# Scores and gates of a mixture of experts turned by VectorE instead of TensorE, with products over six PSUM banks

## The chip, the cores and the metric

The kernel runs on one core of a Trainium2 chip. The metric is the device time of one execution in microseconds (us). The engines are named as in the profile: PE is TensorE (PEld its weight loads), DVE is VectorE, ACT is ScalarE, POOL is GpSimd, SP is SyncE, which here only issues transfers. PSUM has eight banks of 512 fp32 numbers a partition.

## The reference

```python
x = x + L0_ffn(L0_cond(x, ..., itok_B_2_6), ...)     # gated FFN with per-sample adapters, then a linear layer
x = x + L1_ffn(L1_cond(x, W, b, coeff, mask), A, B, Wr)

def L1_ffn(x, A, B, Wr):           # 64 experts of rank 16, the top 16 of each token count
    scores = xf @ Wr.T                                    # 1024 tokens x 64 experts
    top_vals, top_idx = jax.lax.top_k(scores, 16)
    G = zeros(N, 64).at[rows, top_idx].set(softmax(top_vals))
    h = jnp.einsum('nd,krd->nkr', xf, A)                  # 1024 x 1024
    return 2.0 * jnp.einsum('nkr,kdr->nd', h * G[:, :, None], B)
```

x is 8 x 128 x 512 in fp32. The change touches only the scores, the gates G and the order around `h * G`.

## The kernel before, in words

Everything is kept features-first: a feature or an expert is a partition, a token a column. Each fp32 operand of a large product is split into a high and a low part, and `mm3` multiplies high by high, high by low and low by high (lines 1157 to 1159), so that a product over the depth of 512 (four blocks of 128) is 12 matmuls of 512 columns. ACT makes the high part by a copy (all its copies have line 479), DVE the low part by a subtraction (`low`, line 780), except that POOL makes the low part of the expert weights (`am_low`, line 462, and `bm_low`, line 467).

The end of the kernel, around the change, goes as follows. The order of each engine's queue is written out by hand, and engines wait for each other by semaphores.

- `cond(b)`, for the eight samples, writes bank 0 or 1; DVE adds a bias (`c_bias`, line 1011); PE turns the result in four transposes (`turn`, line 1386) into bank 2 or 3; ACT and DVE split it (`ct_high`, `ct_low`) into `c_hl`.
- `scores(s)` (line 1399), for the two halves s of 512 tokens, multiplies with the router's weights into bank 4. High and low halves of the weights lie beside each other, so 128 rows come out: 64 experts from the high part, 64 from the low part. ACT copies the bank into `s_sb` (`s_copy`). `turn_scores(s)` (line 1408) turns it, four tiles of 128 tokens, by products with `ident2`, two identities on top of each other, which also adds the two 64s. The result lies in bank 5, tokens on partitions.
- DVE copies the scores out (line 1030) and routes: `route_first8` takes the eight largest per token (MAX8, line 1032), subtracts the largest (line 1035, for the exponential that ACT makes in `exponent`, line 671) and strikes the eight out (line 1038); `route_next8` does so with the next eight (lines 1043 to 1048); `route_gates` multiplies, sums and inverts (lines 1052 to 1054), and scales the gates into `gate2`, each twice, in four instructions (line 1058). Within it each step waits for the one before.
- `turn_gates(s)` (line 1417) turns `gate2` in four PE transposes into bank 6, and `gate_copy(s)` (ACT) copies that to `gate_x`: 128 rows of gates, the 64 experts twice.
- `experts(n)`, n from 0 to 15, is a product of 12 matmuls with tile j of the expert weights for half s. `H_ORDER` goes over tiles 0 to 3 for half 0, tiles 0 to 3 for half 1, tiles 4 to 7 for half 0, and tiles 4 to 7 for half 1. The banks are 0 to 3 in turn. Four slots hold split weights (`AM_SLOTS`), so `am_high(4)` on ACT, then `am_low(4)` on POOL, must come before `experts(8)`. `hg_gate(n)` (DVE, line 1114) multiplies the bank with `gate_x` of its half, and `hg_high` (ACT) and `hg_low` (DVE) split the result. `combine` then multiplies with the second expert weights, DVE adds to x (line 1143), and the result is stored.

The queue of ACT behind the last samples reads, in this order: `ct_high(7)`, `exponent(0)`, `am_high(2)`, `am_high(3)`, `s_copy(1)`, `gate_copy(0)`, `exponent(1)`, `hg_high(0)` to `(3)`, `gate_copy(1)`, and then in a loop `am_high(n)` (n from 4 to 7), `hg_high(n)`. SP loads expert tile j + 2 when POOL is done with tile j.

Of the kernel before, what the change touches and what calls it, by code (L numbers as in the profile page):

```python
# [28 lines left out]
F32 = mybir.dt.float32  # L29
F32R = mybir.dt.float32r  # L30
I32 = mybir.dt.int32
ALU = mybir.AluOpType
# [3 lines left out]
P = 128  # L36
BATCH, SEQ, D = 8, 128, 512
T = BATCH * SEQ
KD = D // P
# [29 lines left out]

AM_SLOTS = 4  # L70
H_ORDER = [(j + dj, s) for j in range(0, JT, AM_SLOTS) for s in range(2) for dj in range(AM_SLOTS)]
HALF_TAIL = len(H_ORDER) - AM_SLOTS
LAST_TILES = (JT - 2, JT - 1)
# [3 lines left out]
def build(nc, x_blocks, small_in, mask_w, w_open, w_gu, w_dn, a_gu, a_dn, b_three, b_gu, b_dn,  # L77
          lora_a, lora_b, w0_t, w1_t, bias1, wr_t, a_moe, b_moe, consts, out):
    with ExitStack() as ctx:
# [17 lines left out]

        const_sb = at("const_sb", [P, 464], F32, R_CONST)
        block_mask = const_sb[:, 0:PAIR]
        ident = const_sb[:, PAIR:PAIR + P]  # L100
        ident2 = const_sb[:, PAIR + P:PAIR + P + EXPERTS]
        bias0_sb = const_sb[:, 448:448 + KD]
        lora_w_sb = const_sb[:, 448 + KD:448 + KD + 1]
        coeff_sb = const_sb[:, 448 + KD + 1:448 + KD + 1 + BATCH]
        small = R_CONST + 464 * 4
        small_sb = at("small_sb", [P, 64], I32, small)
# [69 lines left out]
        expo = at("expo", [P, 4, EXPERTS], F32, R_AD + 15 * KB)  # L176
        gate2 = at("gate2", [P, 4, 2, EXPERTS], F32, R_ACT + 54 * KB)
        gate_x = at("gate_x", [P, 2, HALF], F32, R_AD)
# [53 lines left out]
        wr_hi, wr_lo = sem("wr_hi"), sem("wr_lo")  # L232
        s_ready, s_copied, score_ready = sem("s_ready"), sem("s_copied"), sem("score_ready")
        top_step, shifted, exp_done, gate_done = sem("top_step"), sem("shifted"), sem("exp_done"), sem("gate_done")
        gate_tr, late_banks_free = sem("gate_tr"), sem("late_banks_free")
        am_hi, am_lo, h_ready, hg_mul, hg_hi, hg_lo = (sem("am_hi"), sem("am_lo"), sem("h_ready"), sem("hg_mul"),
# [34 lines left out]
        def _(sp):  # L271
# [26 lines left out]
            for b in range(4, 6):  # L298
                load_a(b, dma_a[1])
            sp.dma_start(const_sb[:, PAIR:464], consts[:, PAIR:464]).then_inc(dma_const, 16)  # L300

# [175 lines left out]
        def _(act_e):  # L477
# [187 lines left out]
            def s_copy(s):  # L665
                act_e.wait_ge(s_ready, s + 1)
                copy(s_sb[:], ps[:, 4]).then_inc(s_copied, 1)

# [4 lines left out]
            def gate_copy(s):  # L673
                act_e.wait_ge(gate_tr, s + 1)
                copy(gate_x[:, s], ps[:, 6]).then_inc(late_banks_free, 2)

# [66 lines left out]
            ct_high(BATCH - 1)  # L743
            exponent(0)
            am_high(2)
            am_high(3)

            def hg_high(n):
# [9 lines left out]

            s_copy(1)
            gate_copy(0)  # L760
            exponent(1)
            for n in range(4):
                hg_high(n)
# [14 lines left out]
        def _(dve):  # L778
# [247 lines left out]


            def route_first8(s):
                dve.wait_ge(score_ready, s + 1)
                step(nc.vector.tensor_copy(score[:], ps[:, 5, 0:4 * EXPERTS].rearrange("p (t e) -> p t e", t=4)))  # L1030
                for t in range(4):
                    last = nc.vector.max(top8[:, t, 0], score[:, t])
                step(last)

                nc.vector.tensor_tensor(expo[:], score[:], top8[:, :, 0, 0:1].broadcast_to([P, 4, EXPERTS]),
                                        ALU.subtract).then_inc(shifted, 1)
                for t in range(4):
                    last = nc.vector.match_replace(left1[:, t], top8[:, t, 0], score[:, t], NEG)
                step(last)
# [10 lines left out]
            def route_gates(s):  # L1050
                dve.wait_ge(exp_done, s + 1)
                step(nc.vector.tensor_tensor(left1[:], expo[:], left2[:], ALU.mult))
                step(nc.vector.tensor_reduce(gate_sum[:], left1[:], AX_X, ALU.add))
                step(nc.vector.reciprocal(gate_inv[:], gate_sum[:]))
                if s:
                    dve.wait_ge(gate_tr, s)
                for t in range(4):
                    last = nc.vector.tensor_scalar(
                        gate2[:, t], left1[:, t].unsqueeze(1).broadcast_to([P, 2, EXPERTS]),
                        gate_inv[:, t:t + 1], MOE_SCALE, ALU.mult, ALU.mult)  # L1060
                last.then_inc(gate_done, 1)

# [27 lines left out]
            for b in range(BATCH):  # L1090
                c_bias(b)
                if b + 2 < BATCH:
                    xs_low(b + 2)
                if b == 5:
                    wc_low_half(7, 0)
                    wc_low_half(7, 1)
                if b:
                    ct_low(b - 1)
                if 1 <= b < 5:
                    wc_low_half(5 + (b - 1) // 2, (b - 1) % 2)  # L1100
                if b == 6:
                    route_first8(0)
            ct_low(BATCH - 1)
            route_next8()
            route_gates(0)

            def hg_gate(n):
                j, s = H_ORDER[n]
                dve.wait_ge(h_ready, n + 1)
                dve.wait_ge(late_banks_free, 2 * (s + 1))  # L1110
                if n >= 2:
                    dve.wait_ge(hg_hi, n - 1)
                    dve.wait_ge(hg_lo, n - 1)
                nc.vector.tensor_tensor(hg_raw[:, n % 2], ps[:, n % 4], gate_x[:, s],
                                        ALU.mult).then_inc(hg_mul, 1)
# [39 lines left out]
        def _(pe):  # L1155
# [234 lines left out]
            def scores(s):  # L1390

                pe.wait_ge(ct_hi, 4 * s + 4)
                pe.wait_ge(ct_lo, 4 * s + 4)
                pe.wait_ge(x2_done, 2 * KD)
                pe.wait_ge(wr_hi, 1)
                pe.wait_ge(wr_lo, 1)
                for k in range(KD):
# [6 lines left out]
            def turn_scores(s):  # L1404

                pe.wait_ge(s_copied, s + 1)
                for t in range(4):
                    last = nc.tensor.matmul(ps[:, 5, t * EXPERTS:(t + 1) * EXPERTS], s_sb[:, t * P:t * P + P],  # L1408
                                            ident2, start=True, stop=True)
                last.then_inc(score_ready, 1)  # L1410

            def turn_gates(s):
                pe.wait_ge(gate_done, s + 1)
                if s:
                    pe.wait_ge(late_banks_free, 2)
                for t in range(4):
                    last = nc.tensor.transpose(ps[:, 6, t * P:t * P + P],  # L1417
                                               gate2[:, t].rearrange("p c e -> p (c e)"), ident)
                last.then_inc(gate_tr, 1)

            def experts(n, part=range(KD)):
                j, s = H_ORDER[n]
                pe.wait_ge(am_hi, j + 1)
                pe.wait_ge(am_lo, j + 1)
                if n >= 4:
                    pe.wait_ge(hg_mul, n - 3)
                for k in part:
                    last = mm3(ps[:, n % 4], am_hl[:, j % AM_SLOTS, 0, k], am_hl[:, j % AM_SLOTS, 1, k],
                               c_hl[:, 0, k, halves(s)], c_hl[:, 1, k, halves(s)], k == 0, k == KD - 1)
# [4 lines left out]
            for b in range(1, BATCH):  # L1434
# [18 lines left out]
            experts(5)  # L1453
            turn_gates(1)
            for n in range(6, 2 * JT):
# [16 lines left out]
            for o in range(KD):  # L1472
# [3 lines left out]
                for s in range(2):  # L1476
                    pe.wait_ge(late_banks_free, 2 * o + s + 1)
                    pe.wait_ge(hg_lo, HALF_TAIL + AM_SLOTS * s)
# [8 lines left out]
def constants():  # L1487
# [3 lines left out]
    eye = np.eye(P)  # L1491
    return np.concatenate([LORA_SCALE * own, eye, eye[:, :EXPERTS] + eye[:, EXPERTS:]], 1).astype(np.float32)

# [76 lines left out]
```

## Time and profile before

| | before |
|---|---|
| median of 3 runs | 354.89 us (354.57 to 354.99) |
| the profiled execution, whole time | 354.69 us |
| its span, first to last instruction | 353.0 us |
| PE busy | 349.5 us, 99% |
| PEld busy | 294.4 us, 83% |
| DVE busy | 202.2 us, 57% |
| ACT busy | 144.1 us, 41% |
| POOL busy | 78.0 us, 22% |

Times in the trace count from the start of the span. A timeline row gives the start, the duration, engine, line, operation, tile written and tiles read, their shape, and how many instructions are merged in it; in brackets stands how long the engine sat idle before it and what ended that. Matmuls overlap: one of 512 columns lasts 0.39 us in the trace, and the next starts about 0.23 us after it.

### The profile page before, as it was taken

Reading aid. Unit: us, or ns where it says so; the run is one execution under the profiler, and the core shown is the slowest. Engines: PE = TensorE matmul, PEld = TensorE weight load, DVE = VectorE, ACT = ScalarE, POOL = GpSimd, SP = SyncE. Lnnn points to the kernel's source line nnn. Section 1 sums busy time; section 2 is a strip of 40 time slices with the busy share of each in tenths; the row PEclk is TensorE's granted clock in tenths of the full one; section 3 lists DMA queues with packets and bytes.
Section 4 is the critical chain, followed back from the end, with each engine's and each line's share of the span. In section 5 each row is a group of like instructions: output and inputs, shape, how many; then the busy total and the mean of one; then the engine's idle time right before and its main releaser. Section 6 shows DMA issues by size and latency. Waiting matters only on the chain.

```text
span 353.0 us, 4621 instructions
## 1 busy us (share of the span) xinstructions
PE 349.5 (99%) x1682; PEld 294.4 (83%) x1682; DVE 202.2 (57%) x302; ACT 144.1 (41%) x196; POOL 78.0 (22%) x86
## 2 busy tenths in 40 slices
PE   8999999999999999999999999999999999999997
PEld 8899888888888888888888898888888888888885
DVE  3788755334533453685674565879888878501102
ACT  5577544422442243545464471566352443201100
POOL 2361657863340004000000000000041154002200
PEclk9999999999999999999999999999999999999999
DMA  7943343232120054297219019010052022101011
GB/s 202 323 126 144 114 138 112 78 104 77 52 80 0 0 177 130 79 395 291 59 35 306 3 22 417 38 52 11 0 177 62 0 61 69 51 32 59 30 61 59
DMA packets 14802, 37.31 MB, mean 106 GB/s; under 512 B 2272, under 2 KB 4224, under 8 KB 13504
## 3 DMA queue, kind: packets, MB, share of 16 engines
q1 hardware_dynamic: 11920, 31.18, 25.9%
q0 software_dynamic: 2432, 5.57, 5.5%
q10 hardware_dynamic: 432, 0.33, 0.3%
q8 instruction: 11, 0.18, 0.2%
q14 instruction: 7, 0.06, 0.1%
HBM read 34.97 MB, written 2.10 MB: 105 GB/s over the span
## 4 chain that ended last, share of the span: by engine, by line
PE 99%; DVE 0%; issue 0%
PE ps L1157 29%; PE ps L1158 29%; PE ps L1159 29%; PE ps L1179 3%; PE ps L1309 3%; PE ps L1399 1%; PE ps L1386 1%; PE ps L1194 1%; PE ps L1187 1%; PE ps L1198 1%; PE ps L1202 1%; PE ps L1234 1%; PE ps L1408 0%; PE ps L1417 0%; DVE x L1149 0%
## 5 line engine op out<-in xcount | busy, mean ns | idle before, releaser
L1158 PE MATMUL ps<-x_hl,w_hl 128*128 128x512 f32 x144 | 56.2, 390 | 0.0
L1157 PE MATMUL ps<-x_hl,w_hl 128*128 128x512 f32 x144 | 56.2, 390 | 0.0
L1159 PE MATMUL ps<-x_hl,w_hl 128*128 128x512 f32 x144 | 56.1, 389 | 0.0
L462 POOL TENSOR_TENSOR am_hl<-am_raw,am_hl 128x512 fp32r<-128x512 f32 x8 | 11.0, 1387 | 137.4 <-ACT am_hl L479 137.4
L418 POOL DMA_INDIRECT b_raw<-b_gu,row_of x32 | 32.1, 1003 | 27.7 <-DVE b_st L780 19.6
L800 DVE TENSOR_TENSOR glu<-glu,ps 128x512 f32<-128x512 f32 (+1 forms) x22 | 14.9, 683 | 38.8 <-ACT glu L511 26.0
L1159 PEld LDWEIGHTS ps<-x_hl,w_hl 128*128 128x128 f32 x144 | 27.1, 188 | 5.7
L511 ACT ACTIVATE glu<-ps 128x512 f32<-128x512 f32 (+1 forms) x22 | 12.8, 588 | 46.0 <-PE ps L1179 45.8
L1157 PEld LDWEIGHTS ps<-x_hl,w_hl 128*128 128x128 f32 x144 | 27.1, 188 | 5.4
L1158 PEld LDWEIGHTS ps<-x_hl,w_hl 128*128 128x128 f32 x144 | 27.1, 188 | 5.2
L1158 PE MATMUL ps<-act,wd_hl 128*128 128x512 f32 x80 | 31.2, 390 | 0.0
L1157 PE MATMUL ps<-act,wd_hl 128*128 128x512 f32 x80 | 31.2, 389 | 0.0
L1159 PE MATMUL ps<-act,wd_hl 128*128 128x512 f32 x80 | 31.2, 389 | 0.0
L1143 DVE TENSOR_TENSOR x<-ps,x 128x512 f32<-128x512 f32 x8 | 5.5, 692 | 35.2 <-PE ps L1159 35.2
L1157 PE MATMUL ps<-c_hl,am_hl 128*128 128x512 f32 x64 | 25.3, 396 | 0.0
L1158 PE MATMUL ps<-hg,bm_hl 128*128 128x512 f32 (+2 forms) x66 | 25.3, 384 | 0.0
L1159 PE MATMUL ps<-hg,bm_hl 128*128 128x512 f32 (+2 forms) x66 | 25.3, 383 | 0.0
L1157 PE MATMUL ps<-hg,bm_hl 128*128 128x512 f32 (+2 forms) x66 | 25.3, 383 | 0.0
L1159 PE MATMUL ps<-c_hl,am_hl 128*128 128x512 f32 x64 | 25.0, 390 | 0.0
L1158 PE MATMUL ps<-c_hl,am_hl 128*128 128x512 f32 x64 | 24.9, 390 | 0.0
L780 DVE TENSOR_TENSOR act<-glu,act 128x512 f32 (+2 forms) x22 | 15.6, 711 | 16.3 <-ACT act L479 16.1
L989 DVE TENSOR_TENSOR wc_raw<-wc_raw,w_raw 128x2048 f32<-128x2048 f32 x8 | 18.3, 2292 | 7.4 <-ACT wc_raw L630 7.4
(151 smaller groups left out, 729.0 us busy)
## 6 DMA issues: line engine op xcount, KB each, us to landing
wc_raw<-mask_w SPq DMA_DIRECT2D x8, 1024.0 KB, 7.0
w_raw<-w_gu SPq DMA_DIRECT2D x8, 512.0 KB, 3.3
wd_raw<-w_dn SPq DMA_DIRECT2D x10, 256.0 KB, 2.7
w_raw<-w_t SPq DMA_DIRECT2D x2, 1024.0 KB, 7.3
x<-x_blocks SPq DMA_DIRECT2D x2, 1024.0 KB, 6.3
am_raw<-a_moe SPq DMA_DIRECT2D x8, 256.0 KB, 2.8
bm_raw<-b_moe SPq DMA_DIRECT2D x4, 512.0 KB, 3.6
x_raw<-x_blocks SPq DMA_DIRECT2D x7, 256.0 KB, 6.7
```

Of the source, the lines that this page charges most:

```text
L418: nc.gpsimd.indirect_dma_start(b_raw[f % 2][0:F_LAST, p].rearrange("q m f -> q (m f)"), None, b_gu, bass.IndirectOffsetOnAxis(ap=row_of[0: ...
L462: nc.gpsimd.tensor_tensor(am_hl[:, j % AM_SLOTS, 1], am_raw[:, j % 2], am_hl[:, j % AM_SLOTS, 0].bitcast(F32), ALU.subtract).then_inc(am_l ...
L511: nc.scalar.activation(glu[rows, slot], ps[rows, bank], ACT.Silu).then_inc(silu_done, 1)
L780: return nc.vector.tensor_tensor(out, whole, high.bitcast(F32), ALU.subtract)
L800: nc.vector.tensor_tensor(glu[rows, slot], glu[rows, slot], ps[rows, bank], ALU.mult).then_inc(glu_done, 1)
L989: nc.vector.tensor_tensor(wc[:], wc[:], w1_raw[:], ALU.add).then_inc(wc_added, 1)
L1143: nc.vector.tensor_tensor(x2[:, o, half], ps[:, 4 + n % 4], x2[:, o, half], ALU.add)\
L1157: nc.tensor.matmul(out, w_high, m_high, start=start, stop=False)
L1158: nc.tensor.matmul(out, w_high, m_low, start=False, stop=False)
L1159: return nc.tensor.matmul(out, w_low, m_high, start=False, stop=stop)
L1179: last = nc.tensor.matmul(ps[0:cols, bank, h * PAIR:h * PAIR + PAIR], stack[0:F_LAST, 2 * s + h, m, 0:cols], t_st[0:F_LAST, 2 * s + h, m], ...
L1309: last = nc.tensor.matmul(ps[:, 4 + g], stack, act_part(f, h, g * HALF, HALF)[rows], start=(n == 0 and h == 0), stop=(n == FT - 1 and h == 1))
```

## The change: what it does

- **Scores.** `turn_scores` on PE is gone, with `ident2` and 64 columns of constants. ACT copies only rows 64 to 127 of bank 4. DVE adds rows 0 to 63 of the bank to them (`sum_scores`) and turns the sum itself by 32x32 blocks: for each 32 experts four instructions, each of 32 partitions and 4 x 32 columns (`turn_scores`, now DVE's). For half 0 the first 32 experts are turned behind the sum, at b == 6, and the other 32 after `ct_low(7)`; `route_first8(0)`, which stood at b == 6, stands behind them.
- **Gates.** `turn_gates` on PE is gone. DVE scales the gates in one instruction into `gate_tok` (single, no longer twice), and turns them in eight instructions straight into rows 0 to 63 of `gate_x`. `gate_copy` copies these to rows 64 to 127.
- **Banks.** With banks 5 and 6 free, `experts(n)` goes over six banks, 0, 1, 2, 3, 6, 7, and waits for `hg_gate(n - 6)` instead of `hg_gate(n - 4)`.
- **Order.** On DVE `route_first8(1)` moves behind `hg_gate(0)` and `(1)`, and `hg_gate(3)` moves ahead of `route_gates(1)`. On ACT `am_high(2)` and `(3)` stand ahead of `exponent(0)`, and `hg_high(0)` and `(1)` ahead of `exponent(1)`.

```diff
+BLOCK = 32
+H_BANKS = (0, 1, 2, 3, 6, 7)
             def s_copy(s):
                 act_e.wait_ge(s_ready, s + 1)
-                copy(s_sb[:], ps[:, 4]).then_inc(s_copied, 1)
+                copy(s_sb[EXPERTS:P], ps[EXPERTS:P, 4]).then_inc(s_copied, 1)
             def gate_copy(s):
-                act_e.wait_ge(gate_tr, s + 1)
-                copy(gate_x[:, s], ps[:, 6]).then_inc(late_banks_free, 2)
+                act_e.wait_ge(gate_turned, s + 1)
+                copy(gate_x[EXPERTS:P, s], gate_x[0:EXPERTS, s]).then_inc(late_banks_free, 2)
...
             ct_high(BATCH - 1)
-            exponent(0)
             am_high(2)
             am_high(3)
+            exponent(0)
...
             s_copy(1)
             gate_copy(0)
+            for n in range(2):
+                hg_high(n)
             exponent(1)
-            for n in range(4):
+            for n in range(2, 4):
                 hg_high(n)
             gate_copy(1)
...
+            def sum_scores(s):
+                dve.wait_ge(s_copied, s + 1)
+                nc.vector.tensor_tensor(s_sb[0:EXPERTS], ps[0:EXPERTS, 4], s_sb[EXPERTS:P], ALU.add).then_inc(s_summed, 1)
+                dve.wait_ge(s_summed, s + 1)
+
+            def turn_scores(e):
+                summed = s_sb[e:e + BLOCK].rearrange("p (t q n) -> p t q n", t=4, n=BLOCK)
+                for q in range(P // BLOCK):
+                    last = nc.vector.transpose(score[q * BLOCK:q * BLOCK + BLOCK, :, e:e + BLOCK], summed[:, :, q])
+                step(last)
             def route_first8(s):
-                dve.wait_ge(score_ready, s + 1)
-                step(nc.vector.tensor_copy(score[:], ps[:, 5, 0:4 * EXPERTS].rearrange("p (t e) -> p t e", t=4)))
...
-                if s:
-                    dve.wait_ge(gate_tr, s)
-                for t in range(4):
-                    last = nc.vector.tensor_scalar(
-                        gate2[:, t], left1[:, t].unsqueeze(1).broadcast_to([P, 2, EXPERTS]),
-                        gate_inv[:, t:t + 1], MOE_SCALE, ALU.mult, ALU.mult)
-                last.then_inc(gate_done, 1)
+                step(nc.vector.scalar_tensor_tensor(gate_tok[:], left1[:], MOE_SCALE,
+                                                    gate_inv[:].unsqueeze(2).broadcast_to([P, 4, EXPERTS]),
+                                                    ALU.mult, ALU.mult))
+                for e in range(0, EXPERTS, BLOCK):
+                    turned = gate_x[e:e + BLOCK, s].rearrange("p (t q n) -> p t q n", t=4, n=BLOCK)
+                    for q in range(P // BLOCK):
+                        last = nc.vector.transpose(turned[:, :, q],
+                                                   gate_tok[q * BLOCK:q * BLOCK + BLOCK, :, e:e + BLOCK])
+                last.then_inc(gate_turned, 1)
...
                 if b == 6:
-                    route_first8(0)
+                    sum_scores(0)
+                    turn_scores(0)
             ct_low(BATCH - 1)
+            turn_scores(BLOCK)
+            route_first8(0)
             route_next8()
             route_gates(0)
...
-            route_first8(1)
+            sum_scores(1)
+            for e in range(0, EXPERTS, BLOCK):
+                turn_scores(e)
             hg_gate(0)
             hg_gate(1)
+            route_first8(1)
             hg_low(0)
             route_next8()
             hg_low(1)
             hg_gate(2)
+            hg_gate(3)
             route_gates(1)
             hg_low(2)
-            hg_gate(3)
             hg_low(3)
...
             def experts(n, part=range(KD)):
-                if n >= 4:
-                    pe.wait_ge(hg_mul, n - 3)
+                if n >= len(H_BANKS):
+                    pe.wait_ge(hg_mul, n - len(H_BANKS) + 1)
...
                 turn(b - 1)
-                if b == 6:
-                    turn_scores(0)
...
             experts(1)
-            turn_scores(1)
-            turn_gates(0)
             pe.wait_ge(ct_lo, BATCH)
             experts(2)
             experts(3)
             experts(4)
             experts(5)
-            turn_gates(1)
```

## Rows read from the trace of the kernel before

**Rows 1.** The page: busy time, and the chain that ended last.

```profile
PE 349.5 (99%) x1682; PEld 294.4 (83%) x1682; DVE 202.2 (57%) x302; ACT 144.1 (41%) x196; POOL 78.0 (22%) x86
...
PE 99%; DVE 0%; issue 0%
```

**Rows 2.** Windows: stage, busy time of PE, PEld, DVE, ACT, POOL, clock, DMA.

```profile
249.00:267.00 18.00, 18.00 (x95) 15.11 (x94) 15.31 (x45) 7.89 (x13) 5.58 (x4) 1.00 0.31 103
```

**Rows 3.** PE's timeline around the eight pieces that are removed.

```profile
251.17 0.60 PE L1386 MATMUL ps<-const_sb,c_tok 128*128 128x128 f32 x4
...
251.84 0.39 PE L1158 MATMUL ps<-wc_hl,xs_hl 128*128 128x512 f32 x1
...
254.37 0.60 PE L1386 MATMUL ps<-const_sb,c_tok 128*128 128x128 f32 x4
...
255.93 0.40 PE L1158 MATMUL ps<-wc_hl,xs_hl 128*128 128x512 f32 x1
...
266.43 0.39 PE L1159 MATMUL ps<-c_hl,am_hl 128*128 128x512 f32 x1
...
268.17 0.39 PE L1158 MATMUL ps<-c_hl,am_hl 128*128 128x512 f32 x1
...
278.64 0.39 PE L1159 MATMUL ps<-c_hl,am_hl 128*128 128x512 f32 x1
...
279.54 0.40 PE L1158 MATMUL ps<-c_hl,am_hl 128*128 128x512 f32 x1
```

**Rows 4.** PE's timeline: `turn(7)`, and the first matmul of `experts(8)`.

```profile
259.61 0.60 PE L1386 MATMUL ps<-const_sb,c_tok 128*128 128x128 f32 x4
...
284.80 0.39 PE L1157 MATMUL ps<-c_hl,am_hl 128*128 128x512 f32 x1
```

**Rows 5.** ACT's timeline: the second `gate_copy`.

```profile
279.56 0.60 ACT L479 ACTIVATE gate_x<-ps 128x512 f32<-128x512 f32 x1 [0.46 <-PE ps L1417]
```

**Rows 6.** POOL's timeline: `am_low(0)` and `(1)` together, then `am_low(4)`.

```profile
256.20 2.73 POOL L462 TENSOR_TENSOR am_hl<-am_raw,am_hl 128x512 fp32r<-128x512 f32 x2 [114.57 <-ACT am_hl L479]
...
280.76 1.30 POOL L462 TENSOR_TENSOR am_hl<-am_raw,am_hl 128x512 fp32r<-128x512 f32 x1 [14.73 <-ACT am_hl L479]
```

**Rows 7.** DVE's timeline, from the first scores to the second gates.

```profile
256.24 0.41 DVE L1030 COPY score<-ps 128x256 f32<-128x256 f32 x1
...
258.73 0.69 DVE L1011 TENSOR_TENSOR c_tok<-ps,bias_sb 128x512 f32<-128x512 f32 x1 [0.16 <-DVE left L1038]
...
260.88 0.69 DVE L780 TENSOR_TENSOR c_hl<-ps,c_hl 128x512 fp32r<-128x512 f32 x1 [0.45 <-ACT c_hl L479]
...
263.48 1.40 DVE L1052 TENSOR_TENSOR left<-expo,left 128x256 f32<-128x256 f32 x1
...
268.15 0.61 DVE L1032 MAX8 top<-score 128x8 f32<-128x64 f32 x4
...
270.03 1.29 DVE L1114 TENSOR_TENSOR hg_raw<-ps,gate_x 128x512 f32<-128x512 f32 x2
...
272.03 0.60 DVE L1043 MAX8 top<-left 128x8 f32<-128x64 f32 x4
...
274.03 0.69 DVE L780 TENSOR_TENSOR hg<-hg_raw,hg 128x512 fp32r<-128x512 f32 x1
274.64 0.68 DVE L1114 TENSOR_TENSOR hg_raw<-ps,gate_x 128x512 f32<-128x512 f32 x1
275.24 0.42 DVE L1052 TENSOR_TENSOR left<-expo,left 128x256 f32<-128x256 f32 x1
275.69 0.42 DVE L1053 TENSOR_REDUCE gate_sum<-left 128x4 f32<-128x256 f32 x1
...
276.36 0.88 DVE L1058 TENSOR_SCALAR gate<-left,gate_inv 128x128 f32<-128x128 f32 x4
```

**Rows 8.** Line 1058 by itself: durations in ns, least, median, most.

```profile
L1058 DVE TENSOR_SCALAR gate<-left,gate_inv x8: 274/280/531, 265.6 to 277.0; 128x128 f32<-128x128 f32 x8
```

**Rows 9.** The tile `am_raw`: DMA time from issue to landing.

```profile
DMA to landing us min/median/max: 2.5/2.8/4.2
```

More of the change, by code:

```diff
@@ L96, in build @@
         assert base + R_ACT + 88 * KB <= nc.sbuf_usable_end
-        const_sb = at("const_sb", [P, 464], F32, R_CONST)
+        const_sb = at("const_sb", [P, 400], F32, R_CONST)
         block_mask = const_sb[:, 0:PAIR]
         ident = const_sb[:, PAIR:PAIR + P]
[L101 to L105, printed above, removed]
+        bias0_sb = const_sb[:, PAIR + P:PAIR + P + KD]
+        lora_w_sb = const_sb[:, PAIR + P + KD:PAIR + P + KD + 1]
+        coeff_sb = const_sb[:, PAIR + P + KD + 1:PAIR + P + KD + 1 + BATCH]
+        small = R_CONST + 400 * 4
         small_sb = at("small_sb", [P, 64], I32, small)
@@ L176, in build @@
         expo = at("expo", [P, 4, EXPERTS], F32, R_AD + 15 * KB)
-        gate2 = at("gate2", [P, 4, 2, EXPERTS], F32, R_ACT + 54 * KB)
+        gate_tok = at("gate_tok", [P, 4, EXPERTS], F32, R_ACT + 54 * KB)
         gate_x = at("gate_x", [P, 2, HALF], F32, R_AD)
@@ L232, in build @@
         wr_hi, wr_lo = sem("wr_hi"), sem("wr_lo")
-        s_ready, s_copied, score_ready = sem("s_ready"), sem("s_copied"), sem("score_ready")
-        top_step, shifted, exp_done, gate_done = sem("top_step"), sem("shifted"), sem("exp_done"), sem("gate_done")
-        gate_tr, late_banks_free = sem("gate_tr"), sem("late_banks_free")
+        s_ready, s_copied, s_summed = sem("s_ready"), sem("s_copied"), sem("s_summed")
+        top_step, shifted, exp_done = sem("top_step"), sem("shifted"), sem("exp_done")
+        gate_turned, late_banks_free = sem("gate_turned"), sem("late_banks_free")
         am_hi, am_lo, h_ready, hg_mul, hg_hi, hg_lo = (sem("am_hi"), sem("am_lo"), sem("h_ready"), sem("hg_mul"),
@@ L299, in _ @@
                 load_a(b, dma_a[1])
-            sp.dma_start(const_sb[:, PAIR:464], consts[:, PAIR:464]).then_inc(dma_const, 16)
+            sp.dma_start(const_sb[:, PAIR:400], consts[:, PAIR:400]).then_inc(dma_const, 16)
             def load_tile(f, slot):
@@ L1113, in hg_gate @@
                     dve.wait_ge(hg_lo, n - 1)
-                nc.vector.tensor_tensor(hg_raw[:, n % 2], ps[:, n % 4], gate_x[:, s],
+                nc.vector.tensor_tensor(hg_raw[:, n % 2], ps[:, H_BANKS[n % len(H_BANKS)]], gate_x[:, s],
                                         ALU.mult).then_inc(hg_mul, 1)
@@ L1396, in scores @@
                 pe.wait_ge(wr_lo, 1)
+                if s:
+                    pe.wait_ge(s_summed, s)
                 for k in range(KD):
@@ L1402, in scores @@
                 last.then_inc(s_ready, 1)
[L1404 to L1419, printed above, removed]
             def experts(n, part=range(KD)):
@@ L1424, in experts @@
                 pe.wait_ge(am_lo, j + 1)
-                if n >= 4:
-                    pe.wait_ge(hg_mul, n - 3)
+                if n >= len(H_BANKS):
+                    pe.wait_ge(hg_mul, n - len(H_BANKS) + 1)
                 for k in part:
-                    last = mm3(ps[:, n % 4], am_hl[:, j % AM_SLOTS, 0, k], am_hl[:, j % AM_SLOTS, 1, k],
+                    last = mm3(ps[:, H_BANKS[n % len(H_BANKS)]], am_hl[:, j % AM_SLOTS, 0, k], am_hl[:, j % AM_SLOTS, 1, k],
                                c_hl[:, 0, k, halves(s)], c_hl[:, 1, k, halves(s)], k == 0, k == KD - 1)
@@ L1476, in _ @@
                 for s in range(2):
-                    pe.wait_ge(late_banks_free, 2 * o + s + 1)
+                    pe.wait_ge(late_banks_free, max(4, 2 * o + s + 1))
                     pe.wait_ge(hg_lo, HALF_TAIL + AM_SLOTS * s)
@@ L1491, in constants @@
     eye = np.eye(P)
-    return np.concatenate([LORA_SCALE * own, eye, eye[:, :EXPERTS] + eye[:, EXPERTS:]], 1).astype(np.float32)
+    return np.concatenate([LORA_SCALE * own, eye], 1).astype(np.float32)
 def rows_of_tiles():
@@ L1558 @@
         "b_moe": a["L1_ffn_B"].transpose(2, 0, 1).reshape(JT, P, KD, P).transpose(2, 1, 0, 3),
-        "consts": columns(464, [constants(), a["L0_ffn_bias"].reshape(KD, P).T,
+        "consts": columns(400, [constants(), a["L0_ffn_bias"].reshape(KD, P).T,
                                 np.repeat(a["L0_ffn_lora_weights"], RANK).reshape(P, 1),
```

## The prediction, as it was put on record before the result was known

> **What bounds the kernel now.** I read the page first, for the engine that is never free, then windows of the end of the kernel, then the timelines of PE, DVE, ACT and POOL there. The page shows PE busy for 99% of the span, and the chain that ended last is 99% PE [rows 1]. The window around the router shows the same: PE 18.00 us of 18.00 at a granted clock of 1.00, the 2.4 GHz level, although DVE is busy for 15.31 us there [rows 2]. So before the change nobody makes PE wait, an instruction taken off PE is worth its time, and one added to DVE costs nothing until it makes PE wait. The question is whether it will: DVE has only 2.7 us free in these 18.
>
> **What PE loses.** I measure each piece as a distance of starts against the same distance without it [rows 3].
> - `turn_scores(0)`: from the start of `turn` to the second matmul behind it is 255.93 - 254.37 = 1.56 us with it, and 251.84 - 251.17 = 0.67 us without. It is worth 0.89 us.
> - `turn_scores(1)` with `turn_gates(0)`: from the last matmul of one product to the second of the next is 268.17 - 266.43 = 1.74 us; two ordinary steps are 0.46. Worth 1.28 us.
> - `turn_gates(1)`: 279.54 - 278.64 = 0.90, less 0.46, is 0.44 us.
>
> Together 2.61 us. If nothing else moved, `experts(8)`, which starts at 284.80 [rows 4], would start at 282.19.
>
> **What `experts(8)` waits for.** It is the first product that needs expert tile 4. ACT makes the high part of that tile behind `gate_copy(1)` in its queue, and POOL the low part. Before, `gate_copy(1)` starts at 279.56 [rows 5] and POOL ends `am_low(4)` at 280.76 + 1.30 = 282.06 [rows 6], 2.74 us ahead of the matmul that wants it. These 2.74 us are all the room there is; taking 2.61 us of PE work away uses nearly all of it. Whatever delays `gate_copy(1)` then delays PE, one for one, and behind it stand `am_high(4)`, POOL's `am_low(4)` and SP's load of tile 6. So I follow the second gates through DVE.
>
> **What one turning instruction costs.** The trace has none. I need the distance T from one to the next in a row of them, each 128 columns. Bounds:
> - Four MAX8 over 64 columns take 0.61 us, 0.15 us each: half the columns, so a floor [rows 7].
> - Four TENSOR_SCALAR over 128 columns, which read and write as many elements per partition, take 0.88 us; one lasts 0.28, so the distance is (0.88 - 0.28) / 3 = 0.20 us [rows 7, 8].
> - The same instruction without any overlap is 0.28 us [rows 8]; and if a turned element took twice the time of a copied one, the distance would be about that of a 256-column instruction, 0.45 us with its wait [rows 7].
>
> I take 0.235 us. The nearest row is the one at 0.20, and a block of 32 columns must have come in before its first turned column can go out: from 256 to 512 columns an instruction grows by 0.69 - 0.42 = 0.27 us [rows 7], 1.05 ns a column, so 32 columns are 0.034 us, an estimate. One instruction then lasts 0.31 us, and a group of four with the wait behind it 3 x 0.235 + 0.31 + 0.04 = 1.055 us. The Trainium skill (VectorE: DVE Perf Modes, "The three transpose paths") gives 311 ns for a 128 x 128 bf16 turn on VectorE; no run here shows it, and by it the sum below would hardly change.
>
> **The path of the second gates, after.** All from [rows 7] unless another group is named.
> - `turn(7)` comes to PE 0.89 us earlier, at 258.72 instead of 259.61 [rows 4]. Its `c_bias(7)` stands on DVE behind the new `sum_scores(0)` and four turns. The sum starts at 256.24 where the copy of the scores stood, costs 0.73 (a 512-column instruction of 0.69 and the wait), the turns 1.055: `c_bias(7)` runs from 258.03 to 258.72. In the trace PE starts 0.19 us behind it (259.61 - 258.73 - 0.69), so PE stands at 258.91, a stall of 0.19. `ct_low(7)` moves with it by -0.70, to 260.18.
> - From there on DVE works without a pause. `ct_low(7)` 0.61, so 260.79; the other four turns 1.055; `route_first8(0)` without its copy 1.88 (270.03 - 268.15); `route_next8` 2.00 (274.03 - 272.03); multiply, sum, invert 1.12 (276.36 - 275.24); scale in one instruction 0.45 (as 275.69 - 275.24) in place of four of 0.88; eight turns 8 x 0.235 = 1.88. That is 269.18.
> - `sum_scores(1)` 0.73; two groups of turns 2.11; `hg_gate(0)` and `(1)` 1.20; `route_first8(1)` 1.88; `hg_low(0)` 0.61; `route_next8` 2.00; `hg_low(1)` 0.61; `hg_gate(2)` and `(3)` 1.20; 1.12 and 0.45 again: 281.09. Eight turns to the end of the last, 7 x 0.235 + 0.31 = 1.955: 283.05.
> - `gate_copy(1)` starts about 0.08 later, at 283.13, against 279.56: +3.57 us. `am_low(4)` ends at 282.06 + 3.57 = 285.63, and with 0.19 for PE to start `experts(8)` stands at 285.82 instead of 284.80: **+1.02 us**, behind a stall of PE of about 3.4 us (282.19 + 0.19 to 285.82).
>
> The 28 turns on this path are 6.6 us of it; each 0.01 us in T moves the end by 0.28 us.
>
> **What else moves, at nothing.** `experts(6)` needs `hg_gate(0)`, done at 272.7, and starts after 276.6; so the six banks hide the late gates as far as banks can. `hg_gate(4)` comes about 4 us later than before, but `experts(10)` is the first to want it, 5.5 us behind `experts(8)`. `am_high(2)` and `(3)` ahead of `exponent(0)` are hidden behind `route_next8`, 2.00 us, before the exponential is read. Tile 7 has no margin: `am_low(5)` would end near 287.6, then a load of up to 4.2 us [rows 9], the copy and `am_low(7)` come to about 293.9, and `experts(11)` is due at 294.0. The products and sums after that have DVE idle most of the time, so the shift stays as it is to the end. The SBUF source of `gate_copy` and fewer rows in the sum change nothing: columns count. POOL can hold DVE up: the same multiply took 1.40 us with POOL at work and 0.42 without [rows 7]. The new order escapes that in `route_gates(0)` (I counted 0.45 for it), but may meet it elsewhere, up to about 1 us once.
>
> **The sum.** 354.69 us of the profiled execution + 1.02 = 355.71; the median of the runs is 0.20 us above that execution, so 355.9 us.
>
> **The rivals.**
> 1. Forecast: T from 0.222 to 0.28, the path of the gates sets `experts(8)`. 355.4 to 357.4 us. Chance 0.50.
> 2. About the same time: T near 0.20, as four TENSOR_SCALAR go. 28 x 0.035 and the shorter last instructions give 1.1 us less: 354.8. What PE gains and what the gates lose cancel out. Chance 0.27, with all T from 0.172 to 0.222.
> 3. Faster, the other side: the turns are quick, or the steps between them are, and the path ends early enough for PE to keep its gain. It decides at a path shorter by 1.02 + 0.7 us, T = 0.172; at the floor of 0.15 the time is 2.4 us below the forecast, 353.5; with the whole of PE's 2.61 us kept, 352.3. For it: the sum has some 30 terms of mine. Against: a row at 128 columns says 0.20. Chance 0.13.
> 4. Turned elements at half pace, T up to 0.45: 28 x 0.215 = 6.0 us more, 362. Between there and the forecast also the case that POOL's work holds turns up as it did the multiply: POOL runs from 256.20 to 258.93 [rows 6], over the first four turns, and could push `c_bias(7)` and all behind it by 0.6 us. 357.4 us and up. Chance 0.07.
> 5. The granted clock falls. PE has stood still nowhere in the router's stage, the clock there is 1.00 [rows 2], and after a stall of 3.4 us it could drop to the 1.2 GHz level. Twelve matmuls at half pace would cost 12 x 0.23 = 2.8 us on top: 358.7. Chance 0.03. The Trainium skill (TensorE: Matmul & The Clock Gate, Part 1) has an idle TensorE fall back to half its clock; the trace of before has no such stall that could show it here.
>
> **How the numbers follow.** A measurement of this kernel tells 0.2%, 0.7 us, from no change. Slower: 0.50 + 0.07 + 0.03 = 0.60; within: 0.27; faster: 0.13. The range leaves out half of the fast case and most of cases 4 and 5: 353.7 to 358.3 us. The forecast's own range is 355.4 to 357.4.
>
> **What would show it.** Right: PE waits once, for POOL's low part of the expert weights, ahead of the ninth product, some 3 us long; PE's matmuls fall by 24, from 1682 to 1658; 32 turning instructions on DVE of about 0.3 us; the second `gate_copy` near 283. Wrong: no wait there (rival 3), turns far from 0.235 us apart, a stall in front of another product, or a fallen clock. What would hurt most is a wrong T, as it counts 28 times.

## The result, and the profile after

The changed kernel takes 361.46 us (median of 6 runs, 361.21 to 362.28) against 354.83 us before (6 runs, 354.57 to 355.25). The ratio is 1.0189, with a 95% interval from 1.0177 to 1.0200: **1.9% slower**. The forecast was 355.9 us, with a range that ended at 358.3.

The page of the changed kernel, its busy line and the chain that ended last, which answer to [rows 1]:

```profile
PE 350.0 (97%) x1658; PEld 293.4 (82%) x1658; DVE 208.5 (58%) x328; ACT 144.4 (40%) x196; POOL 77.5 (22%) x86
...
PE 91%; DVE 7%; issue 2%; ACT 0%; DVEq 0%; ACTq 0%
```

PE has its 24 matmuls fewer, and the kernel does not end earlier. DVE, which had no part in the chain, holds 7% of it. The windows of the same kernel say where (columns as in [rows 2]: PE, PEld, DVE, ACT, POOL, granted clock, DMA):

```profile
249.00:267.00 18.00, 17.76 (x87) 14.44 (x86) 15.64 (x46) 8.11 (x13) 5.11 (x4) 1.00 0.35 117
267.00:285.00 18.00, 15.91 (x71) 12.83 (x69) 17.15 (x63) 3.51 (x6) 0.00 (x0) 1.00 0.00 0
285.00:306.00 21.00, 17.08 (x64) 13.91 (x65) 16.13 (x22) 9.66 (x15) 9.92 (x6) 0.84 0.20 52
```

PE is idle in the second window and the third, DVE is busy for 17.15 of 18 us ahead of that, and the granted clock of the third window is 0.84. PE's timeline there, whose stall stands in front of `experts(8)` and answers to [rows 4]:

```profile
259.32 0.66 PE L1406 MATMUL ps<-const_sb,c_tok 128*128 128x128 f32 x4 [0.24 <-DVE c_tok L1014]
...
282.52 0.39 PE L1179 MATMUL ps<-c_hl,am_hl 128*128 128x512 f32 x1
288.92 0.76 PE L1177 MATMUL ps<-c_hl,am_hl 128*128 128x512 f32 x1 [6.01 <-issue]
289.48 0.63 PE L1178 MATMUL ps<-c_hl,am_hl 128*128 128x512 f32 x1
289.91 0.63 PE L1179 MATMUL ps<-c_hl,am_hl 128*128 128x512 f32 x1
...
294.18 0.52 PE L1177 MATMUL ps<-c_hl,am_hl 128*128 128x512 f32 x1
294.53 0.39 PE L1178 MATMUL ps<-c_hl,am_hl 128*128 128x512 f32 x1
294.76 0.40 PE L1179 MATMUL ps<-c_hl,am_hl 128*128 128x512 f32 x1
```

There are two things to see. PE stands still for 6.0 us, and the 12 matmuls of `experts(8)` then start 0.43 us apart instead of 0.23, which is the 1.2 GHz level; with `experts(9)` the distance is 0.23 again. What PE waited for is named "issue" here, that is, not named. ACT and POOL of the same kernel name it (the rows answer to [rows 5, 6]):

```profile
286.19 0.63 ACT L480 ACTIVATE gate_x<-gate_x 64x512 f32<-64x512 f32 x1 [3.42 <-DVE gate_x L1073]
286.84 0.63 ACT L480 ACTIVATE am_hl<-am_raw 128x512 fp32r<-128x512 f32 x1
```

```profile
287.55 1.27 POOL L463 TENSOR_TENSOR am_hl<-am_raw,am_hl 128x512 fp32r<-128x512 f32 x1 [23.53 <-ACT am_hl L480]
```

POOL ends `am_low(4)` at 287.55 + 1.27 = 288.82, and PE starts 0.10 us later. DVE's timeline shows how the gates got there (it answers to [rows 7]):

```profile
257.29 1.25 DVE L1039 STREAM_TRANSPOSE score<-s_sb 32x128 f32<-32x128 f32 x4
258.58 0.69 DVE L1014 TENSOR_TENSOR c_tok<-ps,bias_sb 128x512 f32<-128x512 f32 x1
...
263.30 1.00 DVE L1047 TENSOR_TENSOR expo<-score,top 128x256 f32<-128x256 f32 x1
...
268.70 2.50 DVE L1073 STREAM_TRANSPOSE gate_x<-gate_tok 32x128 f32<-32x128 f32 x8
271.24 0.68 DVE L1033 TENSOR_TENSOR s_sb<-ps,s_sb 64x512 f32<-64x512 f32 x1
271.95 2.53 DVE L1039 STREAM_TRANSPOSE score<-s_sb 32x128 f32<-32x128 f32 x8
...
283.59 2.50 DVE L1073 STREAM_TRANSPOSE gate_x<-gate_tok 32x128 f32<-32x128 f32 x8
```

Eight turns last 2.50 us: they lie 0.31 us apart, where I had taken 0.235.

**Where the 6.8 us of the span went** (359.8 - 353.0). `experts(8)` starts at 288.92 against 284.80. Of these 4.12 us, 0.22 were there before the change comes into play (the turn at 254.37 stands at 254.59 in this execution), so the change makes 3.90. The slow clock adds 2.55 us over the 12 matmuls: `experts(9)` starts 5.26 us behind `experts(8)` (294.18 - 288.92), where the kernel before took 2.71 us (287.51 - 284.80, with the start of its `experts(9)` below). Together 6.67 of 6.8 us.

```profile
287.51 0.39 PE L1157 MATMUL ps<-c_hl,am_hl 128*128 128x512 f32 x1
```

### The profile page after: what moved, and what is told of

The parts are those of the page before. It is cut to its first block, busy times and chain, and to the rows that moved or that the text cites. A ratio compares the mean times of both kernels' runs of the same rounds, so it can differ in the third digit from the quotient of the medians.

```text
span 359.8 us, 4599 instructions
## 1 busy us (share of the span) xinstructions
PE 350.0 (97%) x1658; PEld 293.4 (82%) x1658; DVE 208.5 (58%) x328; ACT 144.4 (40%) x196; POOL 77.5 (22%) x86
## 4 chain that ended last, share of the span: by engine, by line
PE 91%; DVE 7%; issue 2%; ACT 0%; DVEq 0%; ACTq 0%
PE ps L1177 27%; PE ps L1179 26%; PE ps L1178 26%; PE ps L1199 3%; PE ps L1329 3%; DVE gate_x L1073 1%; DVE score L1039 1%; PE ps L1214 1%; PE ps L1207 1%; PE ps L1406 1%; PE ps L1218 1%; PE ps L1222 1%; PE ps L1254 1%; PE ps L1421 1%; DVE left L1058 0%
## 5 line engine op out<-in xcount | busy, mean ns | idle before, releaser
L463 POOL TENSOR_TENSOR am_hl<-am_raw,am_hl 128x512 fp32r<-128x512 f32 x8 | 10.2, 1284 | 143.1 <-ACT am_hl L480 143.1
L1177 PE MATMUL ps<-c_hl,am_hl 128*128 128x512 f32 x64 | 26.3, 411 | 6.0 <-issue 6.0
L1179 PE MATMUL ps<-c_hl,am_hl 128*128 128x512 f32 x64 | 25.9, 404 | 0.0
L1178 PE MATMUL ps<-c_hl,am_hl 128*128 128x512 f32 x64 | 25.9, 404 | 0.0
```

What stands on the lines that cost most here:

```text
L463: nc.gpsimd.tensor_tensor(am_hl[:, j % AM_SLOTS, 1], am_raw[:, j % 2], am_hl[:, j % AM_SLOTS, 0].bitcast(F32), ALU.subtract).then_inc(am_l ...
L1177: nc.tensor.matmul(out, w_high, m_high, start=start, stop=False)
L1178: nc.tensor.matmul(out, w_high, m_low, start=False, stop=False)
L1179: return nc.tensor.matmul(out, w_low, m_high, start=False, stop=stop)
```

## The experiments

Compare each run by its ratio to the kernel before, timed on the same chip; the changed kernel stands at 1.0189.

**1. The copies of tiles 4 to 7 ahead of the gates.**

```diff
             exponent(1)
+            am_high(4)
+            am_high(5)
             for n in range(2, 4):
                 hg_high(n)
+            am_high(6)
+            am_high(7)
             gate_copy(1)
             for n in range(4, 2 * JT):
-                if 4 <= n < 8:
-                    am_high(n)
                 hg_high(n)
```

> The changed kernel, with am_high(4) to am_high(7) on ACT moved ahead of gate_copy(1): (4) and (5) behind exponent(1), (6) and (7) behind hg_high(3). Theory A, that experts(8) waits only because the split of tile 4 stands behind the late gate_copy(1): the wait of 6.0 us goes, experts(8) starts near 282.8 (against 288.9), the granted clock stays at 1.00, and the time is about 352.6 us, that is 354.8 less the 2.6 us taken off TensorE and plus 0.2 for the stall at turn(7). Theory B, that it is the late gates themselves (hg_gate) or the banks that hold TensorE: a wait of some 3 to 6 us stays in front of experts(8) to (11), the clock still falls, and the time stays above 358 us.

Measured: 353.69 us, ratio 0.9964 (0.9953 to 0.9975). The wait of 6.0 us is gone with nothing else changed, and the clock is 1.00, so theory A holds and theory B falls. The time is 1.1 us above what I expected. PE's waits in the profiled execution:

```profile
PE ps L1179 <- DVE hg_raw L1133: 0.4, 1, 0.4
PE ps L1408 <- DVE c_tok L1016: 0.2, 1, 0.2
```

The first stands in front of `experts(10)`, which waits for the bank that `hg_gate(4)` empties; by the starts of the matmuls it costs 0.5 us, and the other 0.6 us of the 1.1 stay open. DVE's timeline shows why it came late: POOL's two `am_low` ran from 277.48 to 280.34, and the comparison in `route_next8(1)`, 0.42 us elsewhere, ends 0.3 us behind them.

```profile
279.39 1.23 DVE L1062 TENSOR_TENSOR left<-left,score 128x256 f32<-128x256 f32 x1
```

**2. The same, spread out.**

```diff
             exponent(1)
+            am_high(4)
             for n in range(2, 4):
                 hg_high(n)
+            am_high(5)
+            am_high(6)
             gate_copy(1)
             for n in range(4, 2 * JT):
-                if 4 <= n < 8:
-                    am_high(n)
                 hg_high(n)
+                if n == 4:
+                    am_high(7)
```

> The changed kernel with the copies of tiles 4 to 7 ahead of the second gate_copy again, but spread out: am_high(4) behind exponent(1), am_high(5) and (6) behind hg_high(3), am_high(7) behind hg_high(4). In the run with all four moved, POOL's am_low(4) and (5) in one piece held one step of route_next8(1) on VectorE for 0.8 us, and TensorE waited 0.6 us for hg_gate(4) in front of experts(10). If those 0.6 us are POOL's doing, that step takes 0.42 us again, the wait is gone, and the time is 353.1 us against 353.7. If the gates are simply too late for six banks, the wait of 0.6 us stays and the time is 353.7 us.

Measured: 352.69 us, ratio 0.9939 (0.9925 to 0.9953). The comparison takes 0.42 us again and the wait is no longer listed, so POOL had caused it; by the starts, `experts(10)` is 0.1 us late instead of 0.5. This is the fastest kernel of the study, 0.6% faster than the kernel before the change.

```profile
279.56 0.42 DVE L1063 TENSOR_TENSOR left<-left,score 128x256 f32<-128x256 f32 x1
```

```profile
285.00:306.00 21.00, 21.00 (x93) 17.11 (x92) 19.50 (x28) 9.82 (x16) 7.23 (x4) 1.00 0.20 63
```

**3. The kernel before with earlier copies.** Is it the order on ACT by itself that pays?

```diff
-            for n in range(4):
+            for n in range(2):
+                hg_high(n)
+            am_high(4)
+            for n in range(2, 4):
                 hg_high(n)
+            am_high(5)
             gate_copy(1)
             for n in range(4, 2 * JT):
-                if 4 <= n < 8:
+                if 6 <= n < 8:
                     am_high(n)
```

> The kernel before, with am_high(4) moved behind hg_high(1) and am_high(5) behind hg_high(3) on ACT, so ahead of gate_copy(1). There TensorE has no wait for tile 4 (POOL is done 2.7 us ahead), so if the gain of the run with the spread copies over the kernel before comes from the work taken off TensorE, this run gains nothing: 354.9 us, within 0.2%. If the order of the copies is worth something by itself, it shows here as up to 2 us less.

Measured: 354.92 us, ratio 0.9999 (0.9989 to 1.0008). An order of this kind by itself gives nothing; the 2.3 us of experiment 2 need the work taken off PE. The order is not the same as in experiment 2: here tiles 6 and 7 keep their places.

**4. The stall filled with matmuls.** The router's weights `wr_st`, which stay where they are, are multiplied into bank 5, and nobody reads the product.

```diff
             for n in range(6, 2 * JT):
+                if n == 8:
+                    for m in range(24):
+                        nc.tensor.matmul(ps[:, 5], wr_st[:, m % KD].rearrange("p h e -> p (h e)"),
+                                         c_hl[:, 0, m % KD, halves(0)], start=m == 0, stop=m == 23)
                 experts(n)
```

> The changed kernel, with 24 more matmuls of 512 columns between experts(7) and experts(8), written to bank 5, which nobody reads: 24 x 0.2275 = 5.5 us of work that lies inside the stall of 6.0 us. experts(8) starts at the same 288.9. If the stall costs a fallen clock on top of its length (12 matmuls 0.43 us apart instead of 0.23), the clock stays at 1.00 and the time falls by 12 x 0.20 = 2.4 us, to 359.0 us. If the slow matmuls behind the stall have another cause (waits of their own, another engine's traffic), they stay, and the time is 361.4 us or more.

Measured: 359.15 us (358.94 to 361.34), ratio 1.0137 (1.0104 to 1.0171). PE has 5.5 us more to do and the kernel is faster. `experts(8)` starts where it did, and at full pace:

```profile
288.91 0.47 PE L1177 MATMUL ps<-c_hl,am_hl 128*128 128x512 f32 x1 [0.49 <-issue]
289.22 0.40 PE L1178 MATMUL ps<-c_hl,am_hl 128*128 128x512 f32 x1
289.45 0.40 PE L1179 MATMUL ps<-c_hl,am_hl 128*128 128x512 f32 x1
```

So the slow matmuls were the clock's doing, and the fallen clock cost the difference of the medians, 361.46 - 359.15 = 2.3 us, against 2.55 us read from the trace. One of the four executions took 361.34 us, 2.1 us more than the next, at a mean granted clock of 0.999; there is no trace of it, so what it lost is not known.

**5. One more group of turns** on the path, which writes the same numbers once more.

```diff
             sum_scores(1)
             for e in range(0, EXPERTS, BLOCK):
                 turn_scores(e)
+            turn_scores(BLOCK)
```

> The changed kernel with one group of four turns more, a repetition of turn_scores(32) for half 1, which writes the same numbers again. If the turns lie on the path that sets experts(8) one for one, and each costs 0.31 us with no overlap, experts(8) starts 4 x 0.31 + 0.04 = 1.3 us later, near 290.2, and the time is 362.7 us. If another wait ended last, the time is 361.4 us; if turns overlapped as I had forecast, 362.4 us.

Measured: 362.77 us, ratio 1.0220 (1.0203 to 1.0236), 1.3 us above the changed kernel. Counted from `turn(7)`, `experts(8)` starts 30.97 us later against 29.60, 1.37 us more. Here the trace names the wait:

```profile
PE ps L1178 <- POOL am_hl L463: 7.4, 1, 7.4
```

**6. The gates back on PE,** the scores left with DVE. Shortened:

```diff
-                copy(gate_x[EXPERTS:P, s], gate_x[0:EXPERTS, s]).then_inc(late_banks_free, 2)
+                copy(gate_x[:, s], ps[:, 5]).then_inc(late_banks_free, 2)
...
-                for e in range(0, EXPERTS, BLOCK):
-                    turned = gate_x[e:e + BLOCK, s].rearrange("p (t q n) -> p t q n", t=4, n=BLOCK)
...
+                for t in range(4):
+                    last = nc.vector.tensor_scalar(
+                        gate2[:, t], left1[:, t].unsqueeze(1).broadcast_to([P, 2, EXPERTS]),
+                        gate_inv[:, t:t + 1], MOE_SCALE, ALU.mult, ALU.mult)
...
             experts(2)
+            turn_gates(0)
...
+            experts(6)
+            experts(7)
+            turn_gates(1)
```

> The changed kernel with one part undone: the gates are turned by TensorE again (into bank 5, behind experts(2) and experts(7)) and scaled in four instructions; the scores stay with VectorE, and the order on ACT stays. VectorE's path loses two times eight turns of 2.5 us, of which the PE turn, its wait and the four instructions give back 2.4 us: experts(8) starts near 286.3 instead of 288.9, behind a stall of 2.7 us. TensorE does 0.9 us more. If the clock falls only behind a long stall, it holds here, and the time is 361.4 - 2.6 - 2.4 = 356.4 us; if any stall of some us brings it down, 358.8 us. If turning is not what makes the gates late, the time stays above 360 us.

Measured: 357.79 us (356.29 to 358.94), ratio 1.0064 (1.0044 to 1.0085). The stall is 2.7 us as expected, so turning is most of what made the gates late. Counted from `turn(7)`, `experts(8)` starts 27.57 us later against 29.60: 2.0 us earlier than in the changed kernel, 0.6 less than expected, of which POOL holding up the subtraction in `route_first8(0)` for longer (1.31 us instead of 1.00) makes 0.3. The two expected times, 356.4 and 358.8, were for the clock: one execution had a mean granted clock of 1.000 and took 356.29 us, the other three had 0.994 or 0.995 and took 357.60 to 358.94. The length of the stall is known only for the profiled one, 358.94 us. That the others stood still for as long, so that the clock fell or held behind the same stall, is likely but not shown. The clock is not all of the spread either: in the profiled execution nine matmuls take 3.60 us (287.36 to 290.96), 1.6 us more than at full pace, and it is 2.65 us behind the fastest. Its rows:

```profile
287.36 0.47 PE L1175 MATMUL ps<-c_hl,am_hl 128*128 128x512 f32 x1 [2.66 <-ACT am_hl L480]
287.66 0.51 PE L1176 MATMUL ps<-c_hl,am_hl 128*128 128x512 f32 x1
287.97 0.63 PE L1177 MATMUL ps<-c_hl,am_hl 128*128 128x512 f32 x1
...
290.96 0.51 PE L1175 MATMUL ps<-c_hl,am_hl 128*128 128x512 f32 x1
291.30 0.39 PE L1176 MATMUL ps<-c_hl,am_hl 128*128 128x512 f32 x1
```

**7. `hg_gate(3)` back in its old place.**

```diff
             hg_gate(2)
-            hg_gate(3)
             route_gates(1)
             hg_low(2)
+            hg_gate(3)
             hg_low(3)
```

> The changed kernel, with hg_gate(3) back behind route_gates(1) and hg_low(2), as before the change. If the path of the second gates through VectorE sets experts(8) one for one, it starts 0.6 us earlier (288.3), the clock falls all the same, and the time is 360.8 us. If experts(8) waits for something else on another path, the time is 361.4 us.

Measured: 362.50 us, ratio 1.0208 (1.0191 to 1.0225): slower, not faster. I had followed DVE alone. DVE does end its turns 0.4 us earlier, counted from `turn(7)`, but on ACT `hg_high(3)` stands ahead of `gate_copy(1)`, and now waits for a product that DVE makes after the gates:

```profile
286.73 0.63 ACT L480 ACTIVATE hg<-hg_raw 128x512 fp32r<-128x512 f32 x1 [4.69 <-DVE hg_raw L1131]
287.38 0.63 ACT L480 ACTIVATE gate_x<-gate_x 64x512 f32<-64x512 f32 x1
```

The PE stall grows to 7.6 us. So taking gated results 2 and 3 together shortens the path in the changed kernel, by the trace; in the times the two ratios lie 0.2% apart and their intervals overlap, so they alone do not show it.

**8. to 10. Probes of the turn.** Each is the changed kernel with instructions on scratch tiles in DVE's idle time at the end, such as

```diff
+                    for q in range(4):
+                        last = nc.vector.transpose(flat[1][q4[q], 0:128], flat[0][q4[q], 0:128])
```

where `q4[q]` are the 32 partitions from 32 q on.

> The changed kernel with probes on VectorE, in its idle time behind the first four sums into x: turns of 32 x 128, 32 x 64, 32 x 256, 128 x 128, 128 x 256 and 128 x 32, and copies of 32 x 128, four or so in a row. If a turn costs a fixed part and does not overlap the next turn, 32 x 128 lies 0.31 us apart, as 8 in 2.50 us did; with 1.04 ns a column 32 x 64 would be 0.25 and 32 x 256 0.45 apart, and 128 rows cost what 32 do. If a turned element takes longer than a copied one, 32 x 256 is 0.5 us or more and 32 x 64 0.2 or less. The copies lie 0.20 us apart or less. The time of the kernel does not change, 361.4 us.

> The changed kernel with other probes on VectorE in its idle time behind the first three sums into x: four turns of 32 x 128 on the same 32 partitions, four of 64 x 128 on halves in turn, four of 128 x 128; additions of 32 x 128 on changing and on the same partitions, and of 128 x 128. If turns of 32 partitions do not overlap because the partitions change from one to the next, those on the same partitions lie 0.2 us apart like those of 128 rows; if it is the number of rows, they lie 0.31 us apart as before; and if it belongs to any instruction of 32 rows, the additions of 32 rows lie a whole duration apart too, those of 128 rows 0.07 us less. The time does not change, 361.4 us.

> The changed kernel with a third set of probes on VectorE behind the first and the third sum into x: four turns of 32 x 128 with the same input partitions and changing output partitions (as the scores are turned), four with changing input and the same output partitions (as the gates are), four that read partitions 0 to 31 and write 32 to 63 each time, then four MAX8 on changing 32 partitions and four on all 128. In the runs so far turns lay 0.31 us apart when their partitions changed and 0.20 apart when they did not. If either change is enough, the first two sets take 1.25 us each and the third 0.87; if only the output counts, the second takes 0.87 too. If it is so for any instruction, the MAX8 of 32 partitions take a whole duration each, some 0.2 us, and those of 128 rows 0.15. The time does not change, 361.4 us.

Measured times: 361.25, 360.99 and 361.32 us, one execution each. DVE's timeline of the first: four turns of 32 rows on changing partitions (128, 64 and 256 columns), four copies of 32 rows, then two turns of 128 rows.

```profile
319.36 1.24 DVE L1169 STREAM_TRANSPOSE left<-score 32x128 f32<-32x128 f32 x4
320.62 0.99 DVE L1171 STREAM_TRANSPOSE left<-score 32x64 f32<-32x64 f32 x4
...
324.88 1.78 DVE L1175 STREAM_TRANSPOSE expo<-score 32x256 f32<-32x256 f32 x4
326.67 1.91 DVE L1177 COPY left<-score 32x128 f32<-32x128 f32 x4
...
330.31 0.50 DVE L1181 STREAM_TRANSPOSE left<-score 128x128 f32<-128x128 f32 x2
```

The copies were expected 0.20 us apart or less. The first of them took 1.21 us, the others 0.22 each: POOL ran beside it from 325.39 on, and the copy ended 0.1 us behind it. The turns right ahead of it, also beside POOL, were not held up.

```profile
325.39 2.40 POOL L468 TENSOR_TENSOR bm_hl<-bm_raw,bm_hl 128x1024 fp32r<-128x1024 f32 x1 [20.47 <-ACT bm_hl L480]
```

Of the second: 32 rows on the same partitions, 64 rows on halves in turn, 128 rows; then additions of 32 rows on changing partitions, three on the same partitions, and four of 128 rows.

```profile
319.09 0.87 DVE L1171 STREAM_TRANSPOSE left<-score 32x128 f32<-32x128 f32 x4
319.99 1.26 DVE L1174 STREAM_TRANSPOSE left<-score 64x128 f32<-64x128 f32 x4
...
324.60 0.88 DVE L1178 STREAM_TRANSPOSE left<-score 128x128 f32<-128x128 f32 x4
...
330.04 1.17 DVE L1182 TENSOR_TENSOR left<-score,expo 32x128 f32<-32x128 f32 x4
...
331.21 0.68 DVE L1184 TENSOR_TENSOR left<-score,expo 32x128 f32<-32x128 f32 x3
331.93 0.90 DVE L1187 TENSOR_TENSOR left<-score,expo 128x128 f32<-128x128 f32 x4
```

Of the third: only the output partitions change; only the input partitions change; both stay, but differ from each other; MAX8 of 32 rows on changing partitions, and of 128 rows.

```profile
319.35 1.24 DVE L1170 STREAM_TRANSPOSE left<-score 32x128 f32<-32x128 f32 x4
320.62 1.24 DVE L1173 STREAM_TRANSPOSE left<-score 32x128 f32<-32x128 f32 x4
...
330.34 0.88 DVE L1177 STREAM_TRANSPOSE left<-score 32x128 f32<-32x128 f32 x4
331.26 0.92 DVE L1180 MAX8 expo<-score 32x8 f32<-32x64 f32 x4
332.21 0.61 DVE L1183 MAX8 expo<-score 128x8 f32<-128x64 f32 x4
```

What follows: a turn costs what any other instruction of as many columns costs, 0.20 us from one to the next, as long as consecutive instructions keep their partitions. When the partitions of the input or those of the output change from one to the next, the next starts only when the one before has ended. That is not a matter of the number of rows: the turns and additions of 32 rows on the same partitions overlap as those of 128 rows do. The additions do it too, and by the rows MAX8 as well, although MAX8 of 32 rows on the same partitions was not tried. What counts seems to be where the partitions begin: the first turn behind the sum in each probe, 32 rows from partition 0 on, starts 0.60 or 0.61 us behind an addition of 128 rows that lasts 0.69, so it does overlap it.

## Why the prediction was wrong, point by point

- **What PE loses, 2.61 us:** right, within 0.1 us. With no wait left in front of `experts(8)` (experiment 2), the kernel is 2.3 us faster than before: 2.61 less the stall at `turn(7)`. That stall, forecast at 0.19 us, is listed as 0.24, but counted by starts it costs 0.4: `turn(7)` starts 0.63 us behind the last matmul ahead of it, where 0.24 is usual.
- **What `experts(8)` waits for:** right in every link: second gates, `gate_copy(1)`, `am_high(4)`, `am_low(4)`. Experiment 1 takes away the one link on ACT, and the stall goes.
- **What one turning instruction costs:** this step failed. I took 0.235 us from one to the next, out of an instruction of 0.31 us that overlaps the next by 0.075. The turns last 0.30 us and do not overlap. I had read the overlap from instructions that all run on the same 128 partitions [rows 7, 8], while the turns change theirs each time. The extra 0.034 us for filling a block is wrong as well: on the same partitions turns lie 0.20 us apart, as the row said. The sum is also miscounted by one: 32 turns lie on the path, and T counts 27 times in it, not 28. On the path the turns make 27 x (0.313 - 0.235) = 2.1 of the 2.9 us that the forecast of `experts(8)` lacks (288.92 - 0.22 - 285.82): 0.24 and 0.23 us in the two groups of half 0's scores, 0.66 in the first gates, 0.46 in the scores of half 1, 0.54 in the last gates.
- **POOL holding DVE up:** named, "up to about 1 us once", and left out of the sum. It came in `route_first8(0)`: the subtraction took 0.92 us to the next start (263.30 to 264.22) where I had 0.34, behind POOL's `am_low(3)`, which ended at 264.02. That is 0.6 us in the profiled execution; in those of the other runs the same subtraction lasts between 0.75 and 1.48 us.
- **"The SBUF source of `gate_copy` and fewer rows in the sum change nothing":** not quite. Behind `gate_copy(1)` the next copy starts 0.65 us later, where it was 0.50, which is the last 0.15 of the 2.9 us. The source is not the reason: two copies of `am_raw`, from SBUF too, take 1.14 us together, so they overlap. `gate_copy` reads from partition 0 on and writes from partition 64 on, and its neighbours do neither. So this fits what the probes show for DVE, but no run tests it on ACT. The sum of rows 64 to 127 with rows 0 to 63, and the turns that follow `ct_low(7)`, start 0.1 us late, likely for the same reason; about as much is gained elsewhere on the path.

```profile
255.72 1.14 ACT L480 ACTIVATE am_hl<-am_raw 128x512 fp32r<-128x512 f32 x2
```

- **Rival 4, turns held up by POOL:** no. The first four turns ran wholly beside POOL's `am_low(0)` and `(1)` and took the same 1.25 us.
- **Rival 5, the clock:** it happened, for 2.3 us by experiment 4. I gave it 3 in 100 as a case of its own and put it at nothing in the sum. It was no case of its own but a consequence of the stall: the mean granted clock is 0.985 to 0.991 in all 17 executions of the kernels whose profiled execution has a stall of 5.9 us or more, and 0.994 or 0.995 in three of four executions of the kernel with 2.7 us. So with the 3.4 us that the forecast itself had, a fallen clock was already likely. The Trainium skill (TensorE: Matmul & The Clock Gate, Part 1) has an idle TensorE fall back to half its clock, and the trace of the changed kernel agrees: 12 matmuls 0.43 us apart.
- **Tile 7 without margin, the late `hg_gate(4)`, the moved copies of tiles 2 and 3:** none of them made PE wait in the changed kernel. `hg_gate(4)` did so in experiment 1, once the wait in front of `experts(8)` was gone.

The sum with the measured sizes is 355.9 + 2.9 + 2.5 = 361.3 us, against 361.46. The direction and the path were right. Two terms were wrong: the distance of the turns, which I had myself called the term that hurts most (0.31 us for 0.235), and the clock (2.5 us for nothing), the larger of the two. With the turns alone corrected the sum is 358.0 us, still inside the range that ended at 358.3; POOL and ACT make it 358.8, and the clock 361.3.

## What to carry to other kernels

Work taken off the bounding engine is paid only if what the engine needs next is still there in time: follow every link from the slowed engine to the next product, other queues included. Here unrelated copies stood behind the late one in ACT's queue, and moving them turned 1.9% slower into 0.6% faster. When you price a row of small instructions, take the distance from a row whose instructions change partitions in the same way, and price the clock together with the stall, not as a separate accident.

## What the runs showed of the hardware that I had not expected

- On VectorE, 32 x 128 turns lie 0.31 us apart when input or output partitions change from one to the next (4 in 1.24 us) and 0.20 apart when they do not (4 in 0.87 or 0.88); additions 0.29 against 0.20, MAX8 of 64 columns 0.23 against 0.13 (that with 128 rows).
- A turn of 32 rows on changing partitions takes 0.24, 0.30 and 0.44 us for 64, 128 and 256 columns, about 1.03 ns a column over 0.17. Turns of 32 x 256 ran beside POOL's subtraction undisturbed; a copy of 32 x 128 from and to SBUF took 1.21 us beside it instead of 0.22, and a subtraction of 128 x 256 1.00 instead of 0.43.
- Behind a stall of TensorE of 2.7 us (one trace) the granted clock fell, and matmuls started 0.43 us apart for some 3 us, from the third one on; three of four executions of that kernel have a mean granted clock below 1. With 24 matmuls nobody needs in a stall of 6.0 us the clock held, which saved 2.3 us.
